# Context projection, norm, logits, routing and the first shared blocks as one stage of ten steps

## The reference, cut to what matters

```python
x = _layernorm(x + _L0_xattn_ref(...))     # ... out @ Wo.T + bo
x = _layernorm(x + _L0_ffn_ref(x, ...))
# _L0_ffn_ref: E = 8 experts, K = 2 choices, hidden D = 512
scores = jax.nn.softmax(x @ gate_w, axis=-1)
topk_w, topk_idx = jax.lax.top_k(scores, K)
topk_w = topk_w / (jnp.sum(topk_w, axis=-1, keepdims=True) + 1e-20)
for e in range(E):
    hid = jax.nn.silu(x @ w_gate[e]) * (x @ w_up[e])
    y = y + w_per_expert[:, e:e + 1] * (hid @ w_down[e])
shared = jax.nn.silu(x @ ws_gate) * (x @ ws_up) @ ws_down
return (y + shared).reshape(b, s, h)
```

## Time and profile before

| | |
|---|---|
| median of 3 runs | 3049.84 us |
| lowest, highest | 3044.43, 3051.05 us |
| the profiled execution's own time | 3045.06 us |
| its span, first to last instruction | 3043.3 us |
| busy: PE, PEld, DVE, ACT, POOL | 2762.3, 1787.2, 2050.9, 1413.4, 963.9 us |
| mean granted TensorE clock | 0.956 |

### The profile page before, as it was taken

How to read it: one execution, slowest core, us unless ns; L and a number is a source line. 1 busy time by engine, 2 the same in 40 slices (tenths; PEclk the granted TensorE clock), 3 DMA queues, 4 the chain that set the end, 5 groups by cost and what they waited for, 6 DMA issues and landing times. The chain is left out here.

```text
span 3043.3 us, 42715 instructions
## 1 busy us (share of the span) xinstructions
PE 2762.3 (91%) x14144; PEld 1787.2 (59%) x14145; DVE 2050.9 (67%) x3049; ACT 1413.4 (46%) x2550; POOL 963.9 (32%) x986
## 2 busy tenths in 40 slices
PE   7989999999999889999998999759998579999994
PEld 6754445454555345555554555446666459888884
DVE  4568877777777388888887888445665657333337
ACT  2315666666666534444444545423444333233334
POOL 4467630000000044343445455452000330233332
PEclk9978999999999989999999999978999789999997
DMA  6999986363633155555555552255664424313335
GB/s 221 316 241 277 246 215 81 47 81 46 81 49 44 35 125 138 160 163 168 144 145 148 143 143 82 99 148 89 109 109 85 130 93 123 117 52 137 136 125 168
DMA packets 245934, 400.01 MB, mean 131 GB/s; under 512 B 37583, under 2 KB 147767, under 8 KB 244471
## 3 DMA queue, kind: packets, MB, share of 16 engines
q1 hardware_dynamic: 177684, 251.20, 31.6%
q10 hardware_dynamic: 49299, 82.70, 12.8%
q0 software_dynamic: 18768, 63.79, 6.6%
HBM read 231.46 MB, written 166.14 MB: 131 GB/s over the span
## 5 line engine op out<-in xcount | busy, mean ns | idle before, releaser
L655 DVE TENSOR_REDUCE an_m<-an_psm 128x1 f32<-128x1024 f32 x512 | 604.3, 1219 | 165.7 <-PE an_psm L579 164.9
L635 ACT ACTIVATE an_probs<-an_pst 128x512 f32<-128x512 f32 x1024 | 533.9, 604 | 311.5 <-PE an_pst L606 310.2
L1408 ACT ACTIVATE wj_probs<-wj_pst 128x512 f32<-128x512 f32 x512 | 297.8, 595 | 347.4 <-PE wj_pst L1250 339.5
L1125 POOL TENSOR_TENSOR wj_sums<-wj_sums,wj_probs 128x512 f32<-128x512 f32 x192 | 266.2, 1386 | 311.8 <-ACT wj_probs L1408 308.8
L1439 DVE TENSOR_REDUCE wj_m<-wj_pm 128x1 f32<-128x512 f32 x512 | 323.9, 679 | 17.2 <-PE wj_pm L1225 16.8
L579 PE MATMUL an_psm<-an_ks,an_qs 127*128 127x512 f32 x768 | 263.7, 425 | 7.0 <-DVE an_m L655 7.0
L606 PE MATMUL an_pst<-an_qs,an_ks 128*128 128x512 f32 x768 | 253.0, 408 | 5.0 <-ACT an_probs L635 3.3
L1239 PE MATMUL wj_pacc<-wj_probs,wj_vs 128*64 128x512 f32 x1024 | 249.8, 609 | 2.7 <-ACT wj_probs L1408 2.7
L579 PEld LDWEIGHTS an_psm<-an_ks,an_qs 127*128 127x128 f32 x768 | 130.4, 190 | 179.1 <-issue 142.1
L591 PE MATMUL an_pacc<-an_probs,an_vs 128*32 128x512 f32 x1536 | 204.6, 604 | 9.0 <-ACT an_probs L635 8.2
L1250 PE MATMUL wj_pst<-wj_qs,wj_ks 128*128 128x512 f32 x512 | 203.5, 398 | 0.0
(11 more groups left out here) (434 smaller groups left out, 5972.1 us busy)
## 6 DMA issues: line engine op xcount, KB each, us to landing
ew_w<-scr_ws SPq DMA_DIRECT2D x10, 3072.0 KB, 14.3
scr_ws<-wide_pair POOLq DMA_DIRECT2D x27, 1024.0 KB, 5.0
an_qs<-scr_q SPq DMA_DIRECT2D x48, 256.0 KB, 11.8
an_ks<-scr_k SPq DMA_DIRECT2D x48, 256.0 KB, 13.4
ac_qs<-scr_xq ACTq DMA_DIRECT2D x48, 256.0 KB, 5.4
wj_qs<-scr_mq ACTq DMA_DIRECT2D x18, 512.0 KB, 5.1
wj_ks<-scr_mk ACTq DMA_DIRECT2D x18, 512.0 KB, 6.0
scr_xs<-x_acc SPq DMA_DIRECT2D x2, 4128.0 KB, 16.7
```

The costliest lines, as they stand in the source:

```text
L635: act.activation(probs[:, s % 2, j], pst[:, (GH * s + j) % RING], ACT.Exp, scale=HD ** -0.5).then_inc(exp_done, 1)
L655: dve.tensor_reduce(m1[:, hq, col:col + 1], psm[:, n % 2], AX.XY, ALU.max).then_inc(mx_done, 1)
L1125: eng.tensor_tensor(sums[:, x % CPB, j], earlier, probs[:, s % RING, j], ALU.add).then_inc(sum_done[j], 1)
L1408: act.activation(probs[:, x % RING, j], pst[:, j], ACT.Exp, scale=BHD ** -0.5).then_inc(exp_done, 1)
```

## The change

`cross_norm` is deleted, and its work is done inside `run_experts`, in one loop of `NCH + 2` = 10 steps in which step c holds: the logits of chunk c-2, the projection and statistics of chunk c, the multiplication for chunk c+1, the normalisation and the transposes of chunk c-1, and in steps 6, 7 and 8 the shared units 0, 1 and 2 (`LEAD`, `LED`).

- The barrier with its clearing of semaphores between the two stages is gone.
- The low halves of the raw rows (`lower_rows`) are made by GpSimd instead of DVE, out of SBUF, ahead of each chunk's slopes. The multiplication and the residual add work in place.
- The row tiles have two buffers (`c64`) instead of three. SP asks for reciprocals per chunk and not per batch, and asks for the next residual when the old one is normalised (`x_done`), no longer when it is added; later loads stand behind that wait on SP.
- Spread reciprocals, transposes, logits and their transposes share the two banks of one PSUM tile, `ring`. The projection uses the second halves of `py`'s two banks.
- The shared weights are loaded early, behind the wait for the projection's weights; the halves of the rows and the projection's weights lie in the other half of `w`, so expert 0's weights are loaded behind the eighth projection.
- Exp of the scores stands between the Silu of units 2 and 3.
- The routing work moves three units on (`PICK1` at unit 3, groups at 9 to 16, index at 17, experts of tiles at 18), and the inverse of a group is made one unit behind its marks, not two.
- `SH1` is 10 blocks, so 17 units stand between the steps and the tiles, and 6 blocks behind the tiles. `JOINED` is 10, and 6 pairs are left behind the last block.
- The waits of the gathers 3 to 9 are moved to fit.

```diff
@@ cross_norm, removed whole @@
-cross_norm(nc, A, named(craw="xcraw", x1="x1", recip="rself"), ident, xa, xb, acc)
@@ run_experts @@
-SH1 = 3 * SHARED // 4
+SH1 = 5 * SHARED // 8
-        PICK1, PICK2, SHARE, START, PLACE, SPLIT = range(6)
-        INVERT = 3
-        INVERTED = INVERT + NGROUP // 2
-        OWNER = 2 * INVERTED
+        LEAD, LED = 6, 3
+        PICK1, PICK2, SHARE, START, PLACE, SPLIT, MARK = range(LED, LED + 7)
+        INDEX = MARK + NGROUP
+        OWNER = INDEX + 1
+        ring = k.ps("ring", [P, KH, CH])
+        psx, psh = ring[:, 0].rearrange("p (k n) -> p k n", k=KH), ring[:, 1].rearrange("p (f n) -> p f n", f=FB)
+        pl, pt = ring[0:NE, 0], ring[:, 1, 0:NT * NE].rearrange("p (t e) -> p t e", e=NE)
@@ sync @@
+            def load_rows(c):
+                heads, tok = chunk(c)
+                if c >= 2:
+                    sp.wait_ge(cnb_done, KH * (c - 1))
...
+            def load_residual(c):
+                if c >= 3:
+                    sp.wait_ge(x_done, NT * (c - 2))
...
+            load_rows(0)
+            sp.wait_ge(rs_zero, 1)
+            load_reciprocals(0)
...
+            sp.wait_ge(ob_done, 1)
+            load_residual(2)
+            sp.dma_start(w[:, 0], scr["ws"][NE * P:(NE + 1) * P]).then_inc(shared_in, 16)
+            for c in range(NCH):
...
+                if c + 2 < NCH:
+                    load_reciprocals(c + 2)
+                if c + 2 < NCH:
+                    load_rows(c + 2)
+                if c + 3 < NCH:
+                    load_residual(c + 3)
+            sp.wait_ge(projected, NT * NCH)
+            sp.dma_start(w[:, 1], scr["ws"][0:P]).then_inc(experts_in, 16)
@@ gpsimd @@
+            def lower_rows(c):
+                for n in range(KH):
+                    pool.wait_ge(cna_done, KH * c + n + 1)
+                    if c >= 2:
+                        pool.wait_ge(projected, NT * (c - 1))
+                    pool.tensor_tensor(cnb[:, c % 2, n], c64[:, c % 2, n], cna[:, c % 2, n].bitcast(F32), ALU.subtract)\
+                        .then_inc(cnb_done, 1)
...
+            lower_rows(0)
+            pool.wait_ge(obias_in, 16)
+            bias(0)
+            bias(1)
+            for c in range(NCH):
+                if c + 1 < NCH:
+                    lower_rows(c + 1)
+                slopes(c)
+                if c + 2 < NCH:
+                    bias(c + 2)
...
-                    pool.wait_ge(g_ready, FIRST - NX + i)
+                    pool.wait_ge(g_ready, INDEX + i - 2)
@@ tensor @@
+            for c in range(NCH + 2):
+                if c >= 2:
+                    logit(c - 2)
+                if c < NCH:
+                    project(c)
+                if c >= 2:
+                    logit_turn(c - 2)
+                if c + 1 < NCH:
+                    spread(c + 1)
+                for u in unit_of(c):
+                    pe.wait_ge(shared_in, 16)
+                    hidden_unit(u)
+                if 1 <= c <= NCH:
+                    turn_rows(c - 1)
+                for u in unit_of(c):
+                    if u:
+                        down_unit(u - 1)
+            for u in range(LED, FIRST):
+                if u == START:
+                    count()
+                hidden_unit(u)
+                down_unit(u - 1)
+                for g in group_of(u - 1):
+                    invert(g)
+            down_unit(FIRST - 1)
@@ scalar @@
+            upper_rows(0)
+            for c in range(NCH + 2):
+                if c >= 2:
+                    copy_logits(c - 2)
+                if 1 <= c <= NCH:
+                    normalise_rows(c - 1)
+                if c + 1 < NCH:
+                    upper_rows(c + 1)
+                for u in unit_of(c):
+                    gate(u, u % 2)
+                if 1 <= c <= NCH:
+                    take_rows(c - 1)
...
+            for u in range(LED, FIRST):
+                gate(u, u % 2)
+                for g in group_of(u):
+                    name(g)
@@ vector @@
+            for c in range(NCH + 2):
+                if c < NCH:
+                    for tt in range(NT):
+                        add(c, tt)
+                if c >= 2:
+                    take_logits(c - 2)
+                if c + 1 < NCH:
+                    multiply(c + 1)
+                if c < NCH:
+                    spreads(c)
+                if c == 0:
+                    reciprocals()
+                for u in unit_of(c):
+                    shared_hidden(u, u % 2)
+                if 1 <= c <= NCH:
+                    take_rows(c - 1)
+                for u in unit_of(c):
+                    if u and u % 2 == 0:
+                        join_block(u // 2 - 1)
+            scores()
```

546 lines of the change are left out of this document (227 added, 319 removed).

## The result

The kernel after takes 3029.4 us in the median of 12 runs (3020.15 to 3041.08), the kernel before 3047.24 in the median of 12 runs beside them (3036.47 to 3061.47). The ratio is 0.9941, with a 95% interval from 0.9924 to 0.9958. Forecast were 3014 us and a range from 2998 to 3034: faster, as forecast, and inside the range, but only a little over half of what the sum said. It also lies outside the forecast's own 3006 to 3021, in the part of the range that was there for the rivals.

What follows compares the result with a forecast made beforehand. VectorE was nearly the bound in the context projection, PE was full in the tiles, and some windows were nearly empty. Terms -10.8 - 27.7 + 6.4 = -32.1 us on 3045.1 gave 3013.0, stated as 3014, range 2998 to 3034.

Steps and rivals of the forecast that it cites:

- The front: Shared units between scores and tiles: seven fewer save 30 us, table load and low clock cost 2.3; gained 27.7.
- The late gather: First gather before the tiles, leaving 3.9 us behind unit 17's product; landing time over 7 us would show one for one.
- the 2.3 for Exp and a low clock: Front: 1.3 us added for Exp's table load between two Silu's, 1 us for a clock perhaps low on entry.
- the two loops of a step: Joined stage: one loop through GpSimd's slopes, one through PE's logits and projection, each 9.9 us at full clock.
- the joined stage: Projection and norm inside the expert stage: barrier, refill and logits' 17 us gone, steps 1.3 us longer; 10.8 us gained.
- The first step 10 and the weights' load 2: Joined stage's start: first step takes 10 us, early load of shared weights adds 2 (bounds 0 and 7).
- Five steps of 10.7 and one of 11.7: Joined stage's middle: five steps of 10.7 us, then step 6 at 11.7 because transposes stand behind the hidden matmuls.
- I take the 0.91: Granted clock in the steps, from the old sixth step: four fifths of time at 2.4 GHz, 0.8x9.9+0.2x13.9 = 10.7 us.
- The rival of the low clock: Clock stays low in the joined stage: 13.2 us a step, units start at half speed, kernel 3031 us; chance 0.18.
- 16.5 us from the eighth projection to the scores: Joined stage's end: adds, aggregation, slopes, normalisation, transposes, halves, logits and copies sum to 16.5, scores starting at 2485.7.
- 18.5 for two more blocks: Behind the tiles: four more units cost 18.5 us, up to 21 if GpSimd's sums hold DVE up.
- The 8.4 us of the earlier trace: Behind the tiles: DVE's time between products two units apart in a block joining two pairs; PE needs 8.7.

Runs made afterwards that it cites:

- e5: Kernel after with only the upper halves' product in the logits, four of six matmuls left out; 3029.01 us in one run, six steps 60.3 us against 65.4.
- e9: Kernel after with logits behind the projection, spread reciprocals in pg and transposes ahead of the unit; 3025.41 us, ratio 0.9922 to the kernel before.
- e6: Kernel after without the third Newton step of GpSimd's slopes; 3047.17 us in one run, six steps 65.8 us against 65.4.
- e3: Kernel after with the raw rows' low halves back on DVE, behind the statistics; ratio 0.9959 to the kernel before, six steps 65.5 us against 65.4.
- e1: Kernel after with the gate matrix asked for first and its halves and casts made behind the first step's reciprocals; 3024.57 us, ratio 0.992 to the kernel before.
- e4: Kernel after with no shared unit in the steps, all 20 between steps and tiles; 3034.65 us, ratio 0.9948 to the kernel before.
- e2: Kernel after with chunk 7's rows turned ahead of unit 2 and chunk 6's logits copy in the ninth step; ratio 0.9932 to the kernel before.
- e8: Kernel after without GpSimd's sums of second expert results behind the tiles; 3029.54 us in one run, blocks behind 51.7 us against 55.6.
- e11: Kernel after with SH1 back to 12 blocks: 21 units in front, 4 blocks behind the tiles; 3041.51 us, ratio 0.9967 to the kernel before.
- e12: Kernel after with e9's logits order, e1's early gate matrix and low halves on DVE; 3017.79 us, ratio 0.989 to the kernel before.

## Why the prediction was right in sign and half in size

**Right, and in part by luck.** The front: last copy of logits to first tile -28.1 us against -27.7. The late gather that would have shown one for one didn't come. But the 0.4 us is a sum of errors: from the product that carries the first choice to the one six units on it took 27.4 us, not 25.8; the seven units left out saved 29.4, not 30; and the 2.3 for Exp and a low clock were not paid.

Of the two loops of a step, that of the logits, the projection, the adds and the multiplication sets it (e5, e9), and GpSimd's through the slopes does not (e6). At full clock it was forecast at 9.9 us and measured at 9.5. Its last leg was wrong all the same: the sum goes from the multiplication over the raw rows' upper and low halves to the logits, and the logits don't wait for these. They wait for x_b, over transposes and the other halves. Both legs end 3.8 to 3.9 us behind the start of the multiplication at full clock, so the length was right by luck, and the low halves seemed to be in the loop when they were not (e3).

The first tile began at 2580.5, short of the 2587 that was to make the forecast wrong; but the stage had begun 6.6 us early by chance, and without that it is 2587.1. The eighth projection at 2469.9, forecast at 2469, owes the same 6.6 us.

**The term that was mis-sized most: the joined stage, -10.8 forecast, +1.8 measured.** By its own steps:
- *First projection at 2392*, 11.4 us behind the stage's start: 12.5. A miss of 1.1.
- *The first step 10 and the weights' load 2*: 14.4 us. The load may well have its part, as the DMA engines were 0.83 busy; but what PE waited for was the gate matrix's place in DVE's order, with its cast slowed by 1.8 us, a step that the prediction didn't have. e1 takes 3.7 of it away. A miss of 2.4.
- *Five steps of 10.7 and one of 11.7*, 65.2 in sum: 68.9. The step that failed is "I take the 0.91" for the clock: the six steps ran at 0.84, and the five without a unit at 0.77 to 0.84, 0.82 in the mean. By the prediction's own formula 0.82 gives 11.3 us, and from first add to first add the five took 11.1 in the mean. So the clock's part was worked out rightly from a clock that did not come. The rival of the low clock had the mechanism, but its 13.2 us a step was far too much. A miss of 3.7, of which 1 is unit 0's step (12.8 against 11.7).
- *16.5 us from the eighth projection to the scores*: 21.5. The sum took each piece of the chain as if nothing stood ahead of it; chunk 6's logits on ACT (2.1), unit 2 on PE (1.4) and on DVE did. A miss of 5.0. Not all of it is the units': e4, which has none, still took 19.2 there, at a granted clock of 0.76. And e2 shows that the order of one step can't give it back while the unit's matmuls stay ahead of the last logits.

Together 12.2 of the 12.6. e4 prices the units' part: 4.6 to 6.4 us, against 12 to 13 gained in front.

**The tail, +6.4 forecast, +9.2 measured.** The term that was mis-sized is 18.5 for two more blocks: they cost 20.9. That is the case which the prediction priced at up to 21, that GpSimd's sums hold DVE up, and e8 shows that it is this alone: 3.9 us over the six blocks, nothing without the sums. Four blocks behind the tiles hardly feel the same sums: from the last tile's low half they took 34.6 us before and 34.4 in e11, where the pace of e8 gives 34.4. Why three joined blocks hardly lose by the sums and five do is not shown; a likely reason is that DVE comes out of the tiles with time in hand, waiting 1.6 to 2.4 us for PE at its first four products there. The 8.4 us of the earlier trace rows misled: the product ahead of these two came at 2976.23, 10.25 us before the first of them, so 8.4 was a catching up and not the price of a block. The last piece gave 11.7 against 12.1.

**The table loads.** The 1.3 us for Exp's table were not paid. Timeline of ACT in the kernel after:

```profile
2490.90 1.28 ACT L2734 ACT_TABLE_LOAD   x1
2492.52 0.42 ACT L2734 ACTIVATE rs_prob<-rs_prob 128x256 f32<-128x256 f32 x1 [0.34 <-DVE rs_prob L2800]
2493.13 1.28 ACT L2649 ACT_TABLE_LOAD   x1 [0.19 <-PE ex_pg L50]
2494.42 0.60 ACT L2649 ACTIVATE ex_gated<-ex_pg 128x512 f32<-128x512 f32 x1
```

The load ran as soon as the copy of logits before it was done, beside the work on DVE that Exp itself waited for. From the last copy of logits to the product of unit 3 it took 3.7 us, no more than before (3.9). The Trainium skill puts every change of table at about 2.66 us with its drain (ScalarE: Activation LUTs, What ACT_TABLE_LOAD costs); the trace does not agree here: the Silu behind the second load of 1.28 us began 0.01 us after its end.

**GpSimd or DVE.** The Trainium skill's rule against two-input work on GpSimd (GPSIMD Engine Reference, Engine selection) cost nothing in the changed kernel (e3) and 5.3 us over six steps once the logits were out of the loop (e12). GpSimd's low halves took 1.27 us in the median in the changed kernel, where 1.33 had been estimated by the page's factor; DVE's took 0.68 in e12.

**What stays open.** What settles the granted clock in the steps. How the 14.4 us of the first step part between the weights' load and the rest: no run moved that load. Which part of e1's 3.7 us is the matrix and which the cast. Nor was the obvious next edit tried, to put unit 2's matmuls behind the last logits.

## What to carry to other kernels

Two branches of a loop that end at the same time are not both its limit. Find in one turn of the timeline who uses the end of each, and when, before judging an edit; and try the edit again when the order behind it has changed: the same move was worth 0 and then 5.3 us. Work that fills gaps is free only up to the last round; there each filler stands ahead of a chain that nothing else hides, so look at the order of every engine in the last two steps by itself. And one distance on one engine of a pipeline may be a catching up behind a longer one: take the price of a turn over several turns, or on the engine that sets the pace.

## What the runs showed of the hardware

The granted clock of a stretch differs between executions and between turns of the same code: the step that the kernel after and e8 share took 9.5 us at 1.00 and 10.7 to 11.7 at 0.84 to 0.77, more than most of the edits to it brought. A gain of a few microseconds in such a loop has to be read between turns of like clock.

GpSimd and DVE slowed each other, and not only where DVE had two inputs. DVE's cast of the 128x16 gate matrix, which has one, took 1.94 us at 2390.43 beside GpSimd's bias and 0.16 in e1; the casts of 128x512 behind the tiles took 574 ns in the mean beside GpSimd's sums and 427 without. In the other direction GpSimd's operations of 128x4 went from 0.20 to 0.41 and 0.65 us beside DVE's cast and subtraction.
